# TensorE's program for a 64-chunk recurrence written out in full, in place of a loop over two chunks

## What is computed

```python
def step(carry, inp):
    W1c, b1c = carry
    xq, xk, xv, et = inp
    Z1 = xk @ W1c + b1c
    grad = _ln_l2_bwd(Z1, xv - xk, g, bb)
    Attn1 = jnp.tril(xq @ xk.swapaxes(-1, -2))
    b1_bar = b1c - jnp.tril(et) @ grad
    Z1_bar = xq @ W1c - et * Attn1 @ grad + b1_bar
    last_eta = et[..., -1, :, None]
    W1n = W1c - (last_eta * xk).swapaxes(-1, -2) @ grad
    b1n = b1c - (last_eta * grad).sum(-2, keepdims=True)
    return ((W1n, b1n), xq + _ln(Z1_bar, g, bb, EPS_IN))
```

## Time and profile before

| | us |
|---|---|
| median of three runs | 658.64 (655.46 to 660.62) |
| the profiled execution, its own time | 655.9 |
| its span, first to last instruction | 654.1 |
| busy in the span: PE, PEld | 526.5 (80%), 366.0 (56%) |
| busy in the span: DVE, ACT, POOL | 464.2 (71%), 368.1 (56%), 341.9 (52%) |
| granted clock of TensorE, mean | 0.727 |
| VectorE's first L951 to its last | 181.0 to 499.3 |

### The profile page before, as it was taken

The page is one execution under the profiler, slowest core; times in us unless marked ns, Lnnn a source line. Parts: engine busy times, 40 slices in busy tenths (PEclk is TensorE's granted clock), DMA queues, the critical chain, the costliest instruction groups (busy, mean ns, idle before and its releaser), DMA issues. The chain is left out here.

```text
span 654.1 us, 29567 instructions
## 1 busy us (share of the span) xinstructions
PE 526.5 (80%) x12150; PEld 366.0 (56%) x12150; DVE 464.2 (71%) x1436; ACT 368.1 (56%) x1172; POOL 341.9 (52%) x595
## 2 busy tenths in 40 slices
PE   0399988988448888888888888888786699859996
PEld 0143333333437778778777777777674354444552
DVE  6455777888456888888888888888886365527441
ACT  0333333323336777777777788877675277454432
POOL 0368887777234555555555555555654365512333
PEclk9999998999755555555555555555556699979999
DMA  9101111111480000000000000000003300000112
GB/s 348 61 0 37 32 32 28 35 42 41 104 185 4 3 0 1 0 1 1 0 1 1 1 1 0 1 1 1 1 4 155 123 1 1 2 1 26 68 59 109
DMA packets 9861, 24.65 MB, mean 38 GB/s; under 512 B 1845, under 2 KB 2510, under 8 KB 9550
## 3 DMA queue, kind: packets, MB, share of 16 engines
q1 hardware_dynamic: 9806, 24.01, 11.9%
HBM read 11.42 MB, written 4.19 MB: 24 GB/s over the span
## 5 line engine op out<-in xcount | busy, mean ns | idle before, releaser
L789 PE MATMUL PS<-work 32*32 32x32 f32 x4064 | 83.5, 238 | 39.2 <-DVE work L951 32.0
L789 PEld LDWEIGHTS PS<-work 32*32 32x32 f32 x4064 | 79.9, 152 | 49.8 <-issue 47.0
L1024 POOL TENSOR_TENSOR work<-work,mask 128x256 f32<-128x256 f32 x64 | 46.6, 729 | 90.7 <-DVE work L951 73.3
L778 PE MATMUL PS<-work 64*32 64x64 f32 x2048 | 69.5, 309 | 18.0 <-ACT work L1095 14.5
L500 PE MATMUL PS<-X,work 128*128 (+3 forms) x160 | 73.7, 609 | 10.2 <-ACT X L645 9.9
L778 PEld LDWEIGHTS PS<-work 64*32 64x32 f32 x2048 | 55.6, 163 | 25.1 <-issue 23.7
L801 PE MATMUL PS<-work 32*64 32x32 f32 x2016 | 68.4, 292 | 0.9 <-issue 0.9
L801 PEld LDWEIGHTS PS<-work 32*64 32x64 f32 x2016 | 59.7, 216 | 5.2 <-issue 1.1
L500 PEld LDWEIGHTS PS<-X,work 128*128 128x128 f32 (+1 forms) x160 | 26.5, 173 | 52.3 <-issue 51.0
L1008 POOL TENSOR_TENSOR work<-KP,cst 128x256 f32<-128x256 f32 x64 | 39.2, 612 | 25.0 <-DVE work L913 17.6
L423 ACT ACTIVATE X<-X,par (+1 forms) x16 | 12.2, 807 | 70.0 <-DVE X L416 70.0
(11 more groups left out here) (145 smaller groups left out, 1278.4 us busy)
## 6 DMA issues: line engine op xcount, KB each, us to landing
X<-in_x SPq DMA_DIRECT2D x4, 1024.0 KB, 8.2
TK<-KP SPq DMA_DIRECT2D x64, 64.0 KB, 1.9
X<-QP SPq DMA_DIRECT2D x8, 512.0 KB, 9.1
TK<-in_x SPq DMA_DIRECT2D x4, 1024.0 KB, 8.1
out<-TK SPq DMA_DIRECT2D x16, 256.0 KB, 2.2
work<-in_rope SPq DMA_DIRECT2D x2, 512.0 KB, 9.8
cst<-in_consts SPq DMA_DIRECT2D x1, 289.0 KB, 5.1
work<-in_wk SPq DMA_DIRECT2D x1, 256.0 KB, 11.2
```

The lines of the kernel that those rows point to most:

```text
L778: mm = nc.tensor.matmul(PS[HD * a:HD * a + HD, ZB[p], b * ZW:b * ZW + ZW], KT2[p][r:r + 64, k * B + b, :, :].rearrange("p e t -> p (e t)") ...
L789: mm = nc.tensor.matmul(PS[HD * a:HD * a + HD, bank, b * width:b * width + HD], AM[p][HD * a:HD * a + HD, b, part, :, :].rearrange("p e t ...
L1024: nc.gpsimd.tensor_tensor(AM[p].rearrange("p b s e t -> p (b s) e t"), S1[p].unsqueeze(2).broadcast_to([P, 2 * B, E, CS]), mask2.rearrange ...
```

## The change

`run_chunks` is deleted, and TensorE runs its 64 bodies written out like the other engines. All counts in its waits become constants.

```diff
-            def run_chunks(eng, body):
-
-                for c in range(4):
-                    body(c, c % 2)
-                with eng.Fori(2, NC // 2 - 2) as pair:
-                    c = pair * 2
-                    body(c, 0)
-                    body(c + 1, 1)
-                for c in range(NC - 4, NC):
-                    body(c, c % 2)
 
             GAIN_AT, PRE_AT = NC // 2 + 8, NC - 8
...
-                run_chunks(pe, body)
+                for c in range(NC):
+                    body(c, c % 2)
                 pe_mean(pe, 0, True)
```

## The result

The written-out kernel takes 682.34 us (681.93 to 683.33, four runs) against 658.06 us: a ratio of 1.0371, with an interval of 1.0328 to 1.0415. The change costs 24 us. The forecast was 673 us, with a range of 660 to 693.

What follows compares the result with a forecast made beforehand. The chain between chunks bounds the loop; written out, TensorE's code fetch would: 58 chunks at 5.16 us plus 1.6, 15.8 us more, edges included. From 655.9 us that gives 671.7, from the median 674.4; forecast 673, range 660 to 693.

Steps and rivals of the forecast that it cites:

- The bound before: Recurrence: the chain from chunk to chunk sets the pace; TensorE arrives early and waits for the gradient, 32.0 us in all.
- the edges: TensorE's loop branches: each costs 0.10 us a pair of chunks, so removing 27 gains 2.7 us.
- Code as the bound: Written-out recurrence: TensorE's code arrives slower than it is used, 3.85 against 3.60 us a block; 5.16 us a chunk.
- The price of a block: TensorE's code fetch: 256 instructions take 3.85 us to turn around, the next block asked for on entering the last.
- the 15.8 us of the sum: Recurrence: 58 chunks at 5.16 us plus 1.6 us give 300.9 us in place of 285.1, 15.8 us more.
- My own first reading: First chunks: three code blocks take 12.07 us, 4.02 each, including one set of the loop's register instructions.
- Chunk 56: GpSimd's additions stretch two VectorE operations by 2.1 us; a block arriving meanwhile hides perhaps 0.5, so 1.6 is added.
- The first chunks and what lies behind: First stalls and code behind the recurrence: stalls stay, code behind costed at nothing, within 1 us either way.
- The case of code that keeps ahead: Rival: several blocks fetched ahead in straight code, so 3.8 us are gained: 652, or 655 from the median; chance 0.10.
- Mild stalls: Rival: TensorE's wait for the gradient absorbs part of the stalls; 4.96 us a chunk, 660 to 663 us; chance 0.12.
- The 0.55 us of waiting: TensorE's wait for the gradient, some 0.5 us a chunk (32.0 / 58), which could use up stalls.
- The harder case: Rival: code bounds the recurrence at 5.54 us a chunk, 37.8 us more, 694 to 696 us; chance 0.05.

Runs made afterwards that it cites:

- loop4: TensorE's loop body made four chunks in place of two, 14 passes in place of 28, against the kernel before: 656.91 us, ratio 0.9973.
- thin: Written-out kernel with the state update's 16 products replaced by four wide ones, 295 instructions a chunk: 654.67 us, against 648.39 us for its loop.
- full: The written-out kernel of the change itself, 343 instructions a chunk, against the kernel before: 682.34 us, ratio 1.0371.
- fat: Written-out kernel with the bias update's four products split into 16 narrow ones, 391 instructions a chunk: 715.57 us, 55 us over the loop with the same split.
- loop8: TensorE's loop body made eight chunks, in seven passes, against the kernel before: 717.96 us, ratio 1.0889.
- straight kernel: The kernel after the change, TensorE's 64 chunks written out, against the kernel before: 682.34 us, ratio 1.0371.
- fat_loop: The kernel before, loop kept, with the bias update's four wide products split into 16 of 32 columns, 391 instructions a chunk: 660.43 us, ratio 1.0017.

## Why the prediction was right, point by point

**The bound before, and the edges.** The edges were costed at 2.7 us. The change removed them, and their gain is inside the 24.8 us that the net stretch lost. `loop4` agrees in size: 14 edges fewer, two more chunks run for the first time, and 1.6 us less. The sentence that without the edge something else ends later was right too; straight stretches never run under 4.82 us for long.

**Code as the bound.** Right, and shown: 67 packets where there was one, stalls 256 instructions apart, a loss that follows the number of instructions (thin, full, fat), and none where the body stays resident (`loop4`).

**The price of a block, 3.85 us.** This is the term that was mis-sized. In the kernel after it is 3.97 us, which gives 5.32 us a chunk in place of 5.16. Without chunk 56 the mean period is 5.30 us, and 57 chunks take 8.1 us more than costed. That is nearly the whole difference in the stretch between the 15.8 us of the sum and the 24.8 measured; chunk 56 has the other 0.9. Taken block by block from the trace (77 of them), a fetch's start to the end of the stall is 2.51 us, where I read 2.4, and from there to the next fetch's start 1.47, where I read 1.35. The second is uneven. Of 14 blocks that began in the late part of the base's group, the wait for the gradient stood 70 to 86 instructions into six of them, and there the next fetch started 1.90 to 2.76 us after the entry; it stood 92 or more into the other eight, with 1.30 to 1.35 us. So the next block seems to be asked for not at entry, as I wrote, but when the sequencer is some 90 instructions in, and a wait on the way delays it. No run tested this by itself. The fat kernel, which hardly waits, has 3.85 us, the value I took: the turn-around was right, and the waits on top of it were missing. My own first reading, 4.02 us, seems to have had one in it: of its three blocks two took 3.85 us each, and the one of 4.37 was entered 78 matmul and load instructions ahead of the correction's group, with its next fetch 1.94 us behind the entry, like the six above. I put this down to the loop's register instructions.

**Chunk 56.** I kept 1.6 of the 2.1 us. The period there is 7.72 us in the kernel after, against a mean of 5.30 for the others: 2.4 us more. Nothing was hidden.

**The first chunks and what lies behind.** Costed at nothing, within 1 us. It was 1.8 us (26.6 less 24.8).

**The rivals.** The case of code that keeps ahead, by the rule of the Trainium skill ("Runtime: NRT & Kernel Launch", section "Instruction fetch mechanics") that fetching is hidden by slower dispatch, fell: the trace disagrees, with idle time of 0.62 us at a block's end in the mean, and 0.2 us or more at 60 of the 77. The same section of the Trainium skill says that a branch to code outside a window of two pages stalls. The stall agrees with `loop8` and its 4.48 us; the window of two does not, since `loop4` goes back over 5.4 blocks without a stall. The same section of the Trainium skill gives TensorE room for 2048 instructions, eight blocks. The runs fit it: 5.4 blocks stay, 10.8 do not. Mild stalls fell because the chunk absorbs only about half of 0.83 us of stalls. The 0.55 us of waiting that I read from the waits was also a little high: one wait of 3.7 us ahead of the loop is in those 32.0 us, and from 214 us on it is 0.50 a chunk. The harder case (5.54 us a chunk) came closer than I gave it.

## What to carry to other kernels

Before writing a loop out, count instructions, not work: an engine that issues hundreds of small matmuls a step uses up its program faster than one block at a time comes (here 256 instructions in 3.6 us, against 3.85 to 3.97 us), and then a loop whose body stays resident is the faster form, as long as it may be (four chunks beat two, eight lost 59 us). The stretches that a program runs for the first time, before and behind its loop, show in the old trace what writing out will cost. And keep large transfers away from them: here 7.6 us came from one wait on SyncE.

## What the runs showed of the hardware that I had not expected

- The code of TensorE is fetched one block ahead (the next fetch started 1.03 to 2.76 us after a block was entered), though a body of 5.4 blocks can stay resident (`loop4`). Room doesn't make it fetch earlier.
- A way back to a block that is gone cost 6.1 us in the mean (`loop8`), with the target close to a block's end, so that two blocks were waited for. Just ahead of each of the six branches, by 0.3 to 0.5 us, one more block was fetched, and the fetch of the target's block began only about 1.0 us behind the branch and took 3.3 to 3.6 us until TensorE went on, where 2.5 is the mean in the straight kernel. Other targets were not tried.
- Sixteen products of 32 columns took no longer than four of 128 (`fat_loop`: 35.11 us busy in both loops): the count of instructions was free in TensorE's time there, and cost 55 us through the code.
- With 48 instructions fewer a chunk the granted clock rose from 0.50 to 0.54 and 0.55 on average, in the loop and in the straight kernel alike.
